# Pair 1's top rows turned by a DMA transpose instead of by the matmul engine, in a Macaron block on one core

## The chip, the cores and the metric
The kernel runs on one core of a Trainium2 chip. Its time is the device time of one launch in microseconds (us). Of the kernel before, three runs gave 824.76, 825.32 and 825.58 us; the median is 825.32.

## What is computed
x has 2 x 1024 rows of 512 numbers. Two feed-forward steps stand around one attention step, each behind a layernorm:

```python
x = x + 0.5 * ffn(layernorm(x))
x = x + attn(layernorm(x))            # one head of 128, softmax over 1024 keys
x = x + 0.5 * ffn(layernorm(x))
# ffn: (silu(x @ Wg) * (x @ Wu)) @ Wd
# Wg, Wu: 512 x 1376, Wd: 1376 x 512, 4-bit weights with group scales and zeros
```

## The kernel before, in words
The 2048 rows are taken 512 at a time (an "x tile" t, four slices r of 128 rows). Two x tiles make a pair: tiles 0 and 1 are pair 0, tiles 2 and 3 pair 1. The first feed-forward step is pairs 0 and 1, then come the attention tiles 4 to 7, and the second feed-forward step is pairs 2 and 3 (tiles 8 to 11). Every fp32 product is made of three passes over a high and a low part (`passes`, `PASSES`), so each operand of the matmul engine is first split: ScalarE copies the high part, VectorE or GpSimd subtracts it and writes the low part.

Pair 0 is computed plainly. Its second half (`plain_bottom`) takes the 11 blocks i of 128 hidden columns: a gate product, an up product, then silu on ScalarE and the product `h` on VectorE. Beside it runs another job, the making of the weight sums for the later pairs: for each of the 11 weight blocks j (`T_ORDER`: the last block first), SyncE fetches the unpacked weights into `full` (`load_full(j)`, L664), VectorE and GpSimd make `t13` and `t24` (`first_blocks(j)`, `second_blocks(j)`), these are split, and SyncE stores them (`save_t(j)`, L671). VectorE makes `first_blocks(10)`, the last, after the last `h` and ahead of the low part of hidden block 2 of the down product (`plain_lo(1, 2)`). Every engine works its instructions off in the order in which they are written, SyncE's DMA queue too.

The rest of pair 0 is `bottom(0)`, the down product: 11 blocks of 12 matmuls. Between them stand two groups of transposes for pair 1 (`turn_pair(1, 0)` after block 4 and `turn_pair(1, 1)` after block 7). Pairs 1 to 3 use a scheme of seven products on sums of quarter blocks: A11 and A12 are the two column halves of the top x tile (t = 2 for pair 1), A21 and A22 those of the bottom tile (t = 3); each quarter block has two halves kt. For each kt ScalarE splits off the high parts (`tiles_hi`), VectorE makes the sums S1 to S4 and low parts (`x_sum`, `x_lo`, `sum_lo`), GpSimd the low parts of S1 and S2. Then VectorE adds pair 0's residual (`residual(0, 1)`, four instructions on `xres`, L2027), and pair 1 begins: `product_1`, `product_6`, `product_2`, and `product_7`, which waits for VectorE's `middle`, the first sum `u2` of pair 1.

A second way to turn x is in the kernel already, for tiles 4, 5, 10 and 11 (`PLANED`): the normalised rows are copied as two planes of 16-bit halves (`to_planes`, GpSimd), the planes are stored to DRAM (`store_planes`, L633), and one DMA transpose per tile brings them back turned into `xn` (`turn_planes`, L638).

Of the kernel before, what the change touches and what calls it, by code (L numbers as in the profile page):

```python
# [11 lines left out]
U16 = mybir.dt.uint16  # L12
# [4 lines left out]
P = 128  # L17
TOKENS, HID, INTER = 2048, 512, 1376
PACK, BITS, GROUP = 8, 4, 128
ROWS = 512  # L20
RT = ROWS // P
# [22 lines left out]
A21 = 7  # L44
# [1 line left out]
PAIRS = 4  # L46


PLANED = (4, 5, 10, 11)

UNITS = 3 * NT
QSLOTS = 6
# [7 lines left out]


TURN_HALVES = tuple((what, kt) for what in (A21, A22, A11, A12) for kt in range(2))
TURN_TILES = tuple((what, kt) for kt in range(2) for what in (A21, A11, A22, A12))
SPLIT_HALVES = tuple((what, kt) for what in (A22, A11, A12) for kt in range(2))
SPLIT_TILES = tuple((what, kt) for kt in range(2) for what in (A11, A22, A12))
SUM_HALVES = tuple((what, kt) for what in (S1, S3, S2, S4) for kt in range(2))
# [11 lines left out]
def macaron(nc, x, w_qkv, b_qkv, w_o, b_o, packed, scales, zeros, g_idx, ident, shifts, groups, out):  # L78
    ctx = ExitStack()
    with ctx:  # L80
# [5 lines left out]
        def place(name, shape, dtype, offset=None):  # L86

            t = nc.alloc_sbuf_tensor_at(name, shape, dtype, offset=at[0] if offset is None else offset)
            if offset is None:
                at[0] += -(-size_of(shape, dtype) // 32) * 32  # L90
            return t
# [82 lines left out]
        wi = place("wi", [P, HID], BF16, t24_at)  # L174


        planes_first = [place(f"planes_first{n}", [P, 2, HID], U16, at_) for n, at_ in enumerate((t13_at, t24_at))]


# [115 lines left out]
        def sem(name):  # L295
            return ctx.enter_context(nc.semaphore(name))
# [26 lines left out]

        s_silu, s_rhi, s_whi, s_th13, s_th24, s_p1, s_g1, s_g2, s_hhi, s_x21, s_xhi, s_shi = (
            sem(n) for n in ("s_silu", "s_rhi", "s_whi", "s_th13", "s_th24", "s_p1", "s_g1", "s_g2", "s_hhi", "s_x21", "s_xhi", "s_shi"))
        s_ahi, s_qhi, s_qkvhi, s_exp, s_phi, s_ohi, s_out, s_planes = (
            sem(n) for n in ("s_ahi", "s_qhi", "s_qkvhi", "s_exp", "s_phi", "s_ohi", "s_out", "s_planes"))

        s_unp, s_int, s_wf, s_tab, s_oh, s_h, s_rlo, s_t13, s_tlo13 = (
            sem(n) for n in ("s_unp", "s_int", "s_wf", "s_tab", "s_oh", "s_h", "s_rlo", "s_t13", "s_tlo13"))  # L330
# [17 lines left out]
        def plane_rows(t, r):  # L348

            if r == 0:  # L350
                return planes_first[t % 2][:, :, :]
            return xn[:, t % 2, r - 1, :].bitcast(U16).rearrange("p (h c) -> p h c", h=2)

        def planes_made(t, r):
            return RT * PLANED.index(t) + r + 1

        def rows_loaded(t):
            return d_row[t % 2], 16 * ((t + 1) // 2)

        def planes_stored(t):  # L360
            return d_planes[t % 2], 16 * RT * (PLANED.index(t) // 2 + 1)

        def planes_turned(t):
            return d_xT[t % 2], 16 * (PLANED.index(t) // 2 + 1)

        def turned_rows(t, k):

            return xn[:, t % 2, k, :]
# [7 lines left out]

        ROWS_TURNED = 6 * KT

        def turned(q, what, kt):
            return 8 + TURN_TILES.index((what, kt)) + 1 if q == 1 else ROWS_TURNED + TURN_HALVES.index((what, kt)) + 1
# [5 lines left out]

            return 2 * (q - 1) + kt + 1 + (2 if what == A11 else 0)

        def block_rows(what):

            return 10 + (what in (A21, A22))

        def turned_block(what, kt):
            return turned_rows(block_rows(what), kt + (2 if what in (A12, A22) else 0))

        def heads_split(a, j):

# [209 lines left out]
        def _(sp):  # L609
# [3 lines left out]
            def load_residual(k, dram, first, slots=range(RT)):  # L613
                for r in slots:

                    if k:
                        sp.wait_ge(d_st[r], 16 * k)
                    sp.dma_start(xres[:, r, :], dram[first + r * P:first + (r + 1) * P, :]).then_inc(d_res[r], 16)
# [10 lines left out]

            def store_planes(t):  # L630
                for r in range(RT):
                    sp.wait_ge(s_planes, planes_made(t, r))
                    sp.dma_start(planes[t][r * P:(r + 1) * P, :, :], plane_rows(t, r)).then_inc(d_planes[t % 2], 16)  # L633

            def turn_planes(t):
# [106 lines left out]
            load_full(2)  # L742
            save_t(0)
            store_rows(0, stream, 0)
            load_residual(1, x, ROWS)
            for j in range(1, NT):
                if j + 2 < NT:
                    load_full(j + 2)
                save_t(j)

            sp.wait_ge(s_up, 2 * NT)
            for i in (NT - 4, NT - 3, NT - 2, NT - 1):
# [15 lines left out]
            for n in range(NT - 2):  # L768
                if n == 0:

                    sp.wait_ge(s_turn, turned(1, A12, 1))
                    stored(0)
                    load_rows(4, stream, 0)
                    stored(1)
                    load_rows(5, stream, ROWS)
                load_block(n + 2)
                if n in (6, 8):
                    store_planes(4 if n == 6 else 5)
                if n == 7:
                    turn_planes(4)  # L780
# [81 lines left out]
        def _(pe):  # L862
# [261 lines left out]
                        turn_pair(1, 1)  # L1124

            def turn_pair(q, kt):
                pe.wait_ge(s_ln[2], RT)
                pe.wait_ge(s_ln[3], RT)
                if kt:
                    pe.wait_ge(s_x21, copied(q, 0))  # L1130
                turn_block(q, A21, kt)
                if kt:
                    pe.wait_ge(s_xlo, split(q, A11, 0))
                turn_block(q, A11, kt)
                if kt:
                    pe.wait_ge(s_xlo, split(q, A22, 0))
                turn_block(q, A22, kt)
                if kt:
                    pe.wait_ge(s_xlo, split(q, A12, 0))
                turn_block(q, A12, kt)  # L1140

            pe.wait_ge(d_small, 32)
            keep_warm(3)
# [223 lines left out]
        def _(act):  # L1367
# [7 lines left out]
                                   scale=rstd[:, t % 2, r:r + 1]).then_inc(s_ln[t], 1)  # L1375


            def rows_hi(t):
                for k in range(KT):
                    act.wait_ge(s_turn, KT * t + k + 1)  # L1380
                    bank = TURN_BANK[k] if t else 4 + k
                    copy((xT0, xT1)[t][:, 0, k, :], ps[:, bank, :]).then_inc(s_rhi, 1)
# [49 lines left out]
            def plain_bottom():  # L1432
                for i in range(NT):
                    w = width(i)
                    if i == NT - 1:

                        act.wait_ge(s_up, 2 * NT)
                    act.wait_ge(s_gate, NT + i + 1)
                    if i == NT - 4:

                        act.wait_ge(d_kept[NT - 1], ALL_KEPT)
                    act.activation(hidden(i)[0:w, :], ps[0:w, plain_bank(1, i, 0), :], ACT.Silu).then_inc(s_silu, 1)
                    if i == NT - 1:

                        act.wait_ge(s_t13, NT - 1)
                        act.wait_ge(s_t24, 2 * (NT - 1))
                        plain_hi(1, 1)

                    if i:
                        t_blocks_hi(i - 1)  # L1450
                    if i in (5, 6, 8, 9):
                        ln_apply(2 if i < 7 else 3, (0, 1) if i in (5, 8) else (2, 3))
                    if i == 3:
                        plain_hi(1, 0)
                plain_hi(1, 2)
                t_blocks_hi(NT - 1)
# [7 lines left out]
                copy(blk_f[:, S2, 1, kt, :], ps[:, turn_at(2, A11, kt), :]).then_inc(s_x21, 1)  # L1464

            def x_hi(q, what, kt):
                if q == 3:
                    act.wait_ge(*planes_turned(block_rows(what)))
                    src = turned_block(what, kt)
                else:  # L1470
                    act.wait_ge(s_turn, turned(q, what, kt))
                    src = ps[:, turn_at(q, what, kt), :]
                copy(blk[:, what, 0, kt, :], src).then_inc(s_xhi, 1)
# [98 lines left out]
            def t_hi(a, kts):  # L1572

                for k in kts:
                    if a < 2:
                        act.wait_ge(*planes_turned(4 + a))
                        src = turned_rows(4 + a, k)
                    else:
                        act.wait_ge(s_turn, 16 + KT * (a - 2) + k + 1)
                        src = ps[:, TURN_BANK[k], :]  # L1580
                    copy(x_turned(a)[:, 0, k, :], src).then_inc(s_ahi, 1)

# [190 lines left out]
        def _(dve):  # L1773
# [39 lines left out]
            def x_sum(q, what, kt):  # L1813
                def turned_tile(which):

                    if q == 3:
                        dve.wait_ge(*planes_turned(block_rows(which)))
                        return turned_block(which, kt)
                    dve.wait_ge(s_xhi, split(q, which, kt))
                    return ps[:, turn_at(q, which, kt), :]  # L1820

# [25 lines left out]
            def x_lo(q, what, kt):  # L1847
                dve.wait_ge(s_xhi, split(q, what, kt))
                if q == 2 and what == A11:

                    dve.wait_ge(s_x21, copied(2, kt, A11))
                src = turned_block(what, kt) if q == 3 else ps[:, turn_at(q, what, kt), :]
                minus(blk[:, what, 1, kt, :], src, f32(blk[:, what, 0, kt, :])).then_inc(s_xlo, 1)

            def sum_lo(q, what, kt):
# [432 lines left out]
        def _(pool):  # L2288
# [15 lines left out]
            def to_planes(t, tiles=range(RT)):  # L2304

                for r in tiles:
                    if r == 0:

                        if t >= 6:
                            pool.wait_ge(*planes_stored(PLANED[PLANED.index(t) - 2]))  # L2310
                    else:

                        pool.wait_ge(s_planes, planes_made(t, r - 1))
                    pool.wait_ge(s_ln[t], r + 1)
                    pool.tensor_copy(plane_rows(t, r), xn[:, t % 2, r, :].bitcast(U16).rearrange("p (c h) -> p h c", h=2)).then_inc(s_planes, 1)

            def w_lo(u):
                pool.wait_ge(s_whi, u + 1)
# [157 lines left out]
```

## Time and profile before
| what | value |
|---|---|
| median of three runs | 825.32 us |
| the profiled execution | 824.82 us |
| its span, first to last instruction | 822.9 us |
| PE (matmul) busy | 809.3 us, 98% |
| DVE (VectorE) busy | 494.3 us, 60% |
| ACT (ScalarE) busy | 272.5 us, 33% |
| POOL (GpSimd) busy | 271.8 us, 33% |
| granted clock of PE | full in all 40 slices |

PE is the matmul engine, PEld its weight loads, SPq the DMA queue of SyncE. In a list of events a row gives start and duration in us, the engine, the line, the operation with what it writes and reads, how many are merged, and in brackets how long the engine was idle before and what ended the wait. The span is 1.9 us shorter than the execution's own time.

### The profile page before, as it was taken

What the parts mean: (1) busy time and instruction counts of PE and PEld (TensorE: products, weight loads), DVE (VectorE), ACT (ScalarE), POOL (GpSimd) and SP (SyncE); (2) the same over time, 40 slices, a digit from 0 to 9 for tenths busy, and PEclk for the clock granted to TensorE, in tenths of its full rate; (3) what the DMA queues carried; (4) which work ended last, traced back from release to release, by engine and by line L of the source; (5) the groups of instructions that cost most, each with busy time, mean ns of one, the idle gap of its engine ahead of it and who ended that gap; (6) DMA issues with size and microseconds to landing.
All of it is one profiled execution on the core that took longest, in us unless ns stands there. A gap on an engine that the chain in (4) does not pass through costs nothing. (4 is left out here: it accounts for less than half of the span.)

```text
span 822.9 us, 10477 instructions
## 1 busy us (share of the span) xinstructions
PE 809.3 (98%) x3868; PEld 665.1 (81%) x3868; DVE 494.3 (60%) x809; ACT 272.5 (33%) x469; POOL 271.8 (33%) x219
## 2 busy tenths in 40 slices
PE   5999999999999999999999999999999999999998
PEld 4877778878888888788898888888878788888786
DVE  7889945756654543557766896546347743443452
ACT  3433433555211211343656872121123321211221
POOL 6646614651115363203064371064431110110100
PEclk9999999999999999999999999999999999999999
DMA  6899958965754467344053159644767164444131
GB/s 168 261 342 288 325 188 278 348 261 231 266 188 160 135 205 201 102 153 154 1 176 131 40 179 356 232 145 159 233 188 225 52 213 159 133 168 133 29 104 52
DMA packets 92221, 151.43 MB, mean 184 GB/s; under 512 B 42860, under 2 KB 53796, under 8 KB 87178
## 3 DMA queue, kind: packets, MB, share of 16 engines
q1 hardware_dynamic: 85492, 139.36, 50.8%
q10 hardware_dynamic: 5814, 7.17, 2.5%
q0 software_dynamic: 864, 4.23, 2.0%
q8 instruction: 31, 0.51, 0.3%
q14 instruction: 20, 0.16, 0.1%
HBM read 104.30 MB, written 42.17 MB: 178 GB/s over the span
## 5 line engine op out<-in xcount | busy, mean ns | idle before, releaser
L868 PE MATMUL ps<-blk,ring 128*128 128x512 f32 (+1 forms) x1386 | 320.8, 389 | 0.0
L868 PEld LDWEIGHTS ps<-blk,ring 128*128 128x128 f32 (+1 forms) x1386 | 256.7, 185 | 57.9 <-POOL blk L2290 0.3
L875 PE MATMUL ps<-wd,hT 128*128 128x512 f32 (+1 forms) x1056 | 250.8, 391 | 0.4 <-DVE hT L1775 0.3
L875 PEld LDWEIGHTS ps<-wd,hT 128*128 128x128 f32 (+1 forms) x1056 | 197.3, 188 | 43.1 <-DVE hT L1775 0.8
L2355 POOL TENSOR_TENSOR h<-h,u 128x512 f32<-128x512 f32 (+1 forms) x33 | 42.7, 1294 | 300.1 <-ACT h L1505 300.1
L875 PE MATMUL ps<-xT,wp 128*128 128x512 f32 x480 | 114.3, 394 | 0.1
L875 PEld LDWEIGHTS ps<-xT,wp 128*128 128x128 f32 x480 | 91.0, 190 | 20.0 <-issue 0.7
L1778 DVE TENSOR_TENSOR u<-ps,p1s 128x512 f32<-128x512 f32 (+1 forms) x66 | 45.3, 687 | 95.7 <-PE ps L868 95.7
L1505 ACT ACTIVATE h<-h 128x512 f32<-128x512 f32 (+1 forms) x33 | 20.9, 632 | 176.9 <-DVE h L1778 176.9
L1778 DVE TENSOR_TENSOR h<-ps,p1s 128x512 f32<-128x512 f32 (+1 forms) x33 | 22.8, 690 | 63.9 <-PE ps L868 63.9
L1778 DVE TENSOR_TENSOR u<-ps,u 128x512 f32<-128x512 f32 (+1 forms) x66 | 45.6, 691 | 24.6 <-PE ps L868 23.5
L1775 DVE TENSOR_TENSOR hT<-h,hT 128x512 fp32r<-128x512 f32 (+1 forms) x44 | 31.5, 727 | 24.2 <-ACT hT L1369 24.1
L1500 ACT ACTIVATE g<-ps 128x512 f32<-128x512 f32 (+1 forms) x33 | 19.7, 598 | 75.0 <-PE ps L868 75.0
L1369 ACT ACTIVATE hT<-u 128x512 fp32r<-128x512 f32 (+1 forms) x33 | 20.9, 632 | 64.5 <-DVE u L2002 64.5
L2002 DVE TENSOR_TENSOR u<-u,g 128x512 f32<-128x512 f32 (+1 forms) x33 | 39.9, 1208 | 1.1
L1369 ACT ACTIVATE hT<-h 128x512 fp32r<-128x512 f32 (+1 forms) x44 | 27.0, 628 | 38.0 <-PE ps L875 37.9
L2301 POOL TENSOR_SCALAR xn<-xn,mv,rstd 128x512 f32<-128x512 f32 x18 | 38.3, 2136 | 0.5
L2295 POOL TENSOR_TENSOR rstd<-rstd,mhalf 128x4 f32<-128x4 f32 (+1 forms) x13 | 15.1, 1158 | 67.7 <-DVE rstd L1797 67.7
L1775 DVE TENSOR_TENSOR hT<-u,hT 128x512 fp32r<-128x512 f32 (+1 forms) x33 | 23.0, 698 | 23.0 <-ACT hT L1369 23.0
L2027 DVE SCALAR_TENSOR_TENSOR xres<-ps,xres 128x512 f32<-128x512 f32 x32 | 21.6, 689 | 24.8 <-PE ps L875 17.4
L2290 POOL TENSOR_TENSOR blk<-blk_f,blk 128x512 fp32r<-128x512 f32 x12 | 18.1, 1516 | 38.9 <-ACT blk L1369 33.6
L1786 DVE BATCH_NORM_STATS2 stats<-xn 128x6 f32<-128x512 f32 x48 | 30.0, 678 | 0.0
(142 smaller groups left out, 897.5 us busy)
## 6 DMA issues: line engine op xcount, KB each, us to landing
ring<-wsaved SPq DMA_DIRECT2D x29, 1024.0 KB, 5.2
ring<-wsaved SPq DMA_DIRECT2D x33, 768.0 KB, 4.6
wsaved<-wp SPq DMA_DIRECT2D x10, 1024.0 KB, 4.9
stream<-xres SPq DMA_DIRECT2D x32, 256.0 KB, 2.3
xn<-stream SPq DMA_DIRECT2D x8, 1024.0 KB, 6.8
xres<-stream SPq DMA_DIRECT2D x32, 256.0 KB, 3.2
wfull<-wf ACTq DMA_DIRECT2D x20, 256.0 KB, 5.6
wsaved<-wp SPq DMA_DIRECT2D x10, 512.0 KB, 5.1
```

Source lines behind the costliest of these rows:

```text
L868: mm = pe.matmul(ps[0:w, bank, :], ring[:, slot, which, a, kt, 0:w], blk[:, which, b, kt, :], start=not onto and kt == 0 and n == 0, stop= ...
L875: mm = pe.matmul(bank_ap, lhs(a), rhs(b), start=first and n == 0, stop=last and n == 2)
L1369: return act.activation(dst, src, ACT.Copy)
L1500: act.activation(g1[0:w, n % 2, :], ps[0:w, product_bank(n // NT + 1, 0), :], ACT.Silu).then_inc(s_g1, 1)
L1505: act.activation(hidden(i)[0:width(i), :], hidden(i)[0:width(i), :], ACT.Silu).then_inc(s_g2, 1)
L1775: return dve.tensor_tensor(out=dst, in0=a, in1=b, op=ALU.subtract)
L1778: return dve.tensor_tensor(out=dst, in0=a, in1=b, op=ALU.add)
L1786: dve.bn_stats(stats[:, t % 2, r, :], x_rows(t)[:, r, :]).then_inc(s_bn, 1)
L2002: dve.tensor_tensor(out=u2[0:w, n % 2, :], in0=u2[0:w, n % 2, :], in1=g1[0:w, n % 2, :], op=ALU.mult)\
L2027: dve.scalar_tensor_tensor(out=xres[:, r, :], in0=ps[:, down_bank(q, half, r), :], scalar=0.5, in1=xres[:, r, :], op0=ALU.mult, op1=ALU.ad ...
L2301: pool.tensor_scalar(x_rows(t)[:, r, :], x_rows(t)[:, r, :], mv[:, t % 2, r, 0:1], rstd[:, t % 2, r:r + 1], ALU.subtract, ALU.mult).then_i ...
L2355: pool.tensor_tensor(out=hidden(i)[0:w, :], in0=hidden(i)[0:w, :], in1=u3[0:w, n % 2, :], op=ALU.mult).then_inc(s_h2, 1)
```

## The change
x tile 2 (A11 and A12 of pair 1) is added to `PLANED`. Its planes are made by ScalarE in `plain_bottom` at i = 5 and 6, behind the layernorm of the same slices; the plane of slice 0 lies in the place of `xres`. SyncE stores them after `save_t(6)`, and turns them after `save_t(7)`. The four loads of the residual rows of pair 0's second half, which stood behind `store_rows(0)`, stand behind that transpose. `turn_pair` turns A21 and A22 alone; ScalarE and VectorE read A11 and A12 from `xn` in SBUF, where they read PSUM before. The plane counters become one per parity of t.

```diff
-PLANED = (4, 5, 10, 11)
+PLANED = (2, 4, 5, 10, 11)
-TURN_TILES = tuple((what, kt) for kt in range(2) for what in (A21, A11, A22, A12))
+TURN_TILES = tuple((what, kt) for kt in range(2) for what in (A21, A22))
+        planes_early = place("planes_early", [P, 2, HID], U16, xres_at)
+        def by_dma(q, what):
+            return q == 3 or q == 1 and what in (A11, A12)
@@ SyncE, pair 0's second half
             store_rows(0, stream, 0)
-            load_residual(1, x, ROWS)
             for j in range(1, NT):
                 if j + 2 < NT:
                     load_full(j + 2)
                 save_t(j)
+                if j == 6:
+                    store_planes(2)
+                if j == 7:
+                    turn_planes(2)
+                    load_residual(1, x, ROWS)
...
                 if n == 0:
-                    sp.wait_ge(s_turn, turned(1, A12, 1))
+                    sp.wait_ge(s_xlo, split(1, A12, 1))
                     stored(0)
@@ matmul engine
             def turn_pair(q, kt):
-                pe.wait_ge(s_ln[2], RT)
                 pe.wait_ge(s_ln[3], RT)
                 if kt:
                     pe.wait_ge(s_x21, copied(q, 0))
                 turn_block(q, A21, kt)
                 if kt:
-                    pe.wait_ge(s_xlo, split(q, A11, 0))
-                turn_block(q, A11, kt)
-                if kt:
                     pe.wait_ge(s_xlo, split(q, A22, 0))
                 turn_block(q, A22, kt)
-                if kt:
-                    pe.wait_ge(s_xlo, split(q, A12, 0))
-                turn_block(q, A12, kt)
@@ ScalarE
+            def to_planes(t, tiles):
+                for r in tiles:
+                    if r == 0:
+                        act.wait_ge(d_st[0], 16)
+                    else:
+                        act.wait_ge(*planes_made(t, r - 1))
+                    act.wait_ge(s_ln[t], r + 1)
+                    copy(plane_rows(t, r), xn[:, t % 2, r, :].bitcast(U16).rearrange("p (c h) -> p h c", h=2)).then_inc(s_planes[t % 2], 1)
...
                     if i in (5, 6, 8, 9):
                         ln_apply(2 if i < 7 else 3, (0, 1) if i in (5, 8) else (2, 3))
+                    if i in (5, 6):
+                        to_planes(2, (0, 1) if i == 5 else (2, 3))
...
             def x_hi(q, what, kt):
-                if q == 3:
-                    act.wait_ge(*planes_turned(block_rows(what)))
-                    src = turned_block(what, kt)
+                if by_dma(q, what):
+                    act.wait_ge(*planes_turned(block_rows(q, what)))
+                    src = turned_block(q, what, kt)
@@ VectorE, x_lo (x_sum alike)
-                src = turned_block(what, kt) if q == 3 else ps[:, turn_at(q, what, kt), :]
+                src = turned_block(q, what, kt) if by_dma(q, what) else ps[:, turn_at(q, what, kt), :]
```

SyncE's queue in pair 0's second half, before, from `load_full(9)` on (`full<-wfull` is a `load_full`, `wsaved<-wp` a `save_t`, `ring<-wsaved` pair 1's first weights):

```order
L664 DMA full<-wfull 128x1024
L671 DMA wsaved<-wp 128x2048
L664 DMA full<-wfull 128x1024
L671 DMA wsaved<-wp 128x2048 x3
L690 DMA ring<-wsaved 128x2048
```

The same place after, from `load_full(8)` on (`xres<-` are the residual loads):

```order
L672 DMA full<-wfull 128x1024
L679 DMA wsaved<-wp 128x2048
L641 DMA planes<-planes_early 128x1024
L641 DMA planes<-xn 128x1024 x3
L672 DMA full<-wfull 128x1024
L679 DMA wsaved<-wp 128x2048
L646 DMA_TRANSPOSE xn<-planes 128x4x1024
L626 DMA xres<-in_L_attn_x 128x512 x4
L672 DMA full<-wfull 128x1024
L679 DMA wsaved<-wp 128x2048 x3
```

Four plane stores, a transpose and four residual loads now stand between `load_full(8)` and `load_full(10)`, the last one.

VectorE in the second group (kt = 1) of pair 1's blocks, before (`blk_f<-...` are the sums, `blk<-...` the low parts):

```order
L1778 TENSOR_TENSOR blk_f<-ps,blk_f 128x512
L1775 TENSOR_TENSOR blk_f<-ps,blk_f 128x512
L1775 TENSOR_TENSOR blk_f<-blk_f,ps 128x512
L1775 TENSOR_TENSOR hT<-h_52,hT 96x512
L1775 TENSOR_TENSOR blk<-ps,blk 128x512 x2
L1775 TENSOR_TENSOR blk_f<-ps,blk_f 128x512
L1775 TENSOR_TENSOR blk<-ps,blk 128x512
L1775 TENSOR_TENSOR blk<-blk_f,blk 128x512 x2
L2027 SCALAR_TENSOR_TENSOR xres<-ps,xres 128x512 x4
```

The same place after:

```order
L1797 TENSOR_TENSOR blk_f<-ps,blk_f 128x512
L1794 TENSOR_TENSOR blk_f<-xn,blk_f 128x512
L1794 TENSOR_TENSOR blk_f<-blk_f,xn 128x512
L1794 TENSOR_TENSOR hT<-h_52,hT 96x512
L1794 TENSOR_TENSOR blk<-xn,blk 128x512
L1794 TENSOR_TENSOR blk<-ps,blk 128x512
L1794 TENSOR_TENSOR blk_f<-xn,blk_f 128x512
L1794 TENSOR_TENSOR blk<-xn,blk 128x512
L1794 TENSOR_TENSOR blk<-blk_f,blk 128x512 x2
L2046 SCALAR_TENSOR_TENSOR xres<-ps,xres 128x512 x4
```

The order of the work is the same; five operands come from `xn` in SBUF in place of `ps` in PSUM.

## Rows read from the trace of the kernel before

**Rows 1.** The page: span, and busy time of the matmul engine.
```profile
span 822.9 us, 10477 instructions
PE 809.3 (98%) x3868; PEld 665.1 (81%) x3868; DVE 494.3 (60%) x809; ACT 272.5 (33%) x469; POOL 271.8 (33%) x219
```

**Rows 2.** Timeline of PE, 186 to 216 us: start, duration, what.
```profile
190.33 1.91 PE L886 MATMUL ps<-idt,xn 128*128 128x128 f32 x16
191.99 8.43 PE L875 MATMUL ps<-wd,hT 128*128 128x512 f32 x36
200.26 1.91 PE L886 MATMUL ps<-idt,xn 128*128 128x128 f32 x16
...
210.24 6.08 PE L868 MATMUL ps<-blk,ring 128*128 128x512 f32 x26
```

**Rows 3.** Timeline of SyncE's DMA queue, 100 to 220 us.
```profile
134.98 2.33 SPq L618 DMA_DIRECT2D xres<-in_L_attn_x  x4
...
164.07 0.32 SPq L671 DMA_DIRECT2D wsaved<-wp  x1
165.70 0.32 SPq L664 DMA_DIRECT2D full<-wfull  x1
...
170.27 0.32 SPq L664 DMA_DIRECT2D full<-wfull  x1
```

**Rows 4.** The same queue, at the transposes of tiles 4 and 5.
```profile
294.26 1.90 SPq L633 DMA_DIRECT2D planes<-xn  x3
...
306.03 5.92 SPq L638 DMA_TRANSPOSE xn<-planes  x1
...
326.41 4.13 SPq L638 DMA_TRANSPOSE xn<-planes  x1
```

**Rows 5.** All four DMA transposes, from issue to landing.
```profile
DMA to landing us min/median/max: 6.2/7.9/8.0
```

**Rows 6.** DMA issues: count, size, median us to landing; whole span.
```profile
full<-wfull SPq DMA_DIRECT2D x10, 512.0 KB, 4.6
...
planes<-xn SPq DMA_DIRECT2D x12, 256.0 KB, 5.7
```

**Rows 7.** The same of 134 to 146 us alone.
```profile
full<-wfull SPq DMA_DIRECT2D x2, 512.0 KB, 7.8
```

**Rows 8.** Busy time by stretch, granted clock, DMA share, GB/s.
```profile
155.00:160.00 5.00, 5.00 (x24) 4.14 (x23) 3.96 (x11) 3.23 (x6) 4.18 (x5) 1.00 0.89 318
```

**Rows 9.** ScalarE, exponentials of attention: count, busy, mean ns of one.
```profile
L1631 ACT ACTIVATE pr<-ps,nmx 128x1024 f32<-128x1024 f32 x16 | 17.8, 1113 | 7.1 <-DVE nmx L2130 6.7
```

**Rows 10.** Timeline of DVE, 165 to 270 us (the first: 143 to 146).
```profile
144.03 0.69 DVE L1775 TENSOR_TENSOR t<-full 128x512 f32<-128x512 f32 x1 [4.44 <-DMA full<-wfull]
...
179.18 1.62 DVE L1775 TENSOR_TENSOR t<-full 128x512 f32<-128x512 f32 x1
180.71 0.68 DVE L1775 TENSOR_TENSOR hT<-h,hT 128x512 fp32r<-128x512 f32 x1
...
202.57 0.69 DVE L1778 TENSOR_TENSOR blk_f<-ps,blk_f 128x512 f32<-128x512 f32 x1 [1.65 <-ACT blk L1369]
...
205.10 1.28 DVE L1775 TENSOR_TENSOR blk<-ps,blk 128x512 fp32r<-128x512 f32 x2
...
209.82 2.47 DVE L2027 SCALAR_TENSOR_TENSOR xres<-ps,xres 128x512 f32<-128x512 f32 x4
213.25 0.69 DVE L1778 TENSOR_TENSOR u<-ps,p1s 128x512 f32<-128x512 f32 x1 [0.97 <-PE ps L868]
```

**Rows 11.** Timeline of POOL, 165 to 300 us: the first low part of kt = 1.
```profile
204.73 1.62 POOL L2290 TENSOR_TENSOR blk<-blk_f,blk 128x512 fp32r<-128x512 f32 x1 [6.16 <-ACT blk L1369]
```

**Rows 12.** Timeline of DVE at pair 3's blocks, all from `xn`, 622 to 662 us.
```profile
631.17 0.68 DVE L1778 TENSOR_TENSOR blk_f<-xn 128x512 f32<-128x512 f32 x1
...
633.76 2.38 DVE L1775 TENSOR_TENSOR blk<-xn,blk 128x512 fp32r<-128x512 f32 x2
...
640.78 0.68 DVE L1778 TENSOR_TENSOR blk_f<-xn 128x512 f32<-128x512 f32 x1
```

More of the change, by code:

```diff
@@ L325, in macaron @@
             sem(n) for n in ("s_silu", "s_rhi", "s_whi", "s_th13", "s_th24", "s_p1", "s_g1", "s_g2", "s_hhi", "s_x21", "s_xhi", "s_shi"))
-        s_ahi, s_qhi, s_qkvhi, s_exp, s_phi, s_ohi, s_out, s_planes = (
-            sem(n) for n in ("s_ahi", "s_qhi", "s_qkvhi", "s_exp", "s_phi", "s_ohi", "s_out", "s_planes"))
+        s_ahi, s_qhi, s_qkvhi, s_exp, s_phi, s_ohi, s_out = (
+            sem(n) for n in ("s_ahi", "s_qhi", "s_qkvhi", "s_exp", "s_phi", "s_ohi", "s_out"))
+        s_planes = [sem(f"s_planes{n}") for n in range(2)]
         s_unp, s_int, s_wf, s_tab, s_oh, s_h, s_rlo, s_t13, s_tlo13 = (
@@ L350, in plane_rows, with of_parity @@
             if r == 0:
-                return planes_first[t % 2][:, :, :]
+                return (planes_early if t == 2 else planes_first[t % 2])[:, :, :]
             return xn[:, t % 2, r - 1, :].bitcast(U16).rearrange("p (h c) -> p h c", h=2)
+        def of_parity(t):
+            return [u for u in PLANED if u % 2 == t % 2].index(t)
         def planes_made(t, r):
-            return RT * PLANED.index(t) + r + 1
+            return s_planes[t % 2], RT * of_parity(t) + r + 1
         def rows_loaded(t):
@@ L360, in planes_stored @@
         def planes_stored(t):
-            return d_planes[t % 2], 16 * RT * (PLANED.index(t) // 2 + 1)
+            return d_planes[t % 2], 16 * RT * (of_parity(t) + 1)
         def planes_turned(t):
-            return d_xT[t % 2], 16 * (PLANED.index(t) // 2 + 1)
+            return d_xT[t % 2], 16 * (of_parity(t) + 1)
         def turned_rows(t, k):
@@ L375, in hidden @@
             return h2_back[:, NT - 1 - i, :]
-        ROWS_TURNED = 6 * KT
+        ROWS_TURNED = 5 * KT
         def turned(q, what, kt):
@@ L389, in copied, with block_rows, turned_block @@
             return 2 * (q - 1) + kt + 1 + (2 if what == A11 else 0)
[L391 to L396, printed above, removed]
+        def by_dma(q, what):
+            return q == 3 or q == 1 and what in (A11, A12)
+        def block_rows(q, what):
+            return {1: 2, 3: 10}[q] + (what in (A21, A22))
+        def turned_block(q, what, kt):
+            return turned_rows(block_rows(q, what), kt + (2 if what in (A12, A22) else 0))
         def heads_split(a, j):
@@ L631, in store_planes @@
                 for r in range(RT):
-                    sp.wait_ge(s_planes, planes_made(t, r))
+                    sp.wait_ge(*planes_made(t, r))
                     sp.dma_start(planes[t][r * P:(r + 1) * P, :, :], plane_rows(t, r)).then_inc(d_planes[t % 2], 16)
@@ L1578, in t_hi @@
                     else:
-                        act.wait_ge(s_turn, 16 + KT * (a - 2) + k + 1)
+                        act.wait_ge(s_turn, 12 + KT * (a - 2) + k + 1)
                         src = ps[:, TURN_BANK[k], :]
@@ L1814, in turned_tile @@
                 def turned_tile(which):
-                    if q == 3:
-                        dve.wait_ge(*planes_turned(block_rows(which)))
-                        return turned_block(which, kt)
+                    if by_dma(q, which):
+                        dve.wait_ge(*planes_turned(block_rows(q, which)))
+                        return turned_block(q, which, kt)
                     dve.wait_ge(s_xhi, split(q, which, kt))
@@ L2309, in to_planes @@
                         if t >= 6:
-                            pool.wait_ge(*planes_stored(PLANED[PLANED.index(t) - 2]))
+                            pool.wait_ge(*planes_stored(t - 6))
                     else:
-                        pool.wait_ge(s_planes, planes_made(t, r - 1))
+                        pool.wait_ge(*planes_made(t, r - 1))
                     pool.wait_ge(s_ln[t], r + 1)
-                    pool.tensor_copy(plane_rows(t, r), xn[:, t % 2, r, :].bitcast(U16).rearrange("p (c h) -> p h c", h=2)).then_inc(s_planes, 1)
+                    pool.tensor_copy(plane_rows(t, r), xn[:, t % 2, r, :].bitcast(U16).rearrange("p (c h) -> p h c", h=2)).then_inc(s_planes[t % 2], 1)
             def w_lo(u):
```

## The prediction, made before the changed kernel ran
> **What bounds the kernel now.** I read the page first: the matmul engine is busy 98% of the span [rows 1], and its clock was granted in full [rows 8]. So what is taken from this engine's stream counts in full, and what makes it wait does too; work elsewhere counts only where it ends last. The timeline of that engine comes next: at 190.33 and at 200.26 us stand the two groups of 16 transposes that the change halves, with 36 matmuls of the down product behind each, and the first product of pair 1 starts at 210.24 [rows 2]. The reader is to see that nothing idles between these rows. The timelines of SyncE's queue and of VectorE show what must be ready by then [rows 3, 4, 10].
>
> **What is removed: 16 of 32 transposes.** The next matmul starts 191.99 - 190.33 = 1.66 us after 16 transposes began, 0.104 us each [rows 2]. Sixteen go, eight per group, as no other has to be added on this engine: 16 x 0.104 = 1.66 us. This is the whole of what the change can give here, 0.2% of the time. The waits that guarded their PSUM banks go too, but the engine did not idle there.
>
> **ScalarE: four copies of 1024 numbers.** The trace has no such copy on this engine. The nearest row is the exponential of 128x1024 at 1113 ns [rows 9]; I take 1.1 us each, 4.5 us in all, 2.2 us in block 5 and 2.2 in block 6. ScalarE was busy 3.23 of 5 us at 155 to 160 us [rows 8], which holds its two layernorm slices, so a block of 5.4 us nearly fills. The matmul engine asks for the `h` of two blocks ago, so a slip of up to 5 us costs it nothing; cost 0, with the planes made near 158 us. Were the copies at twice the length, they would still be ready near 162 us, about when SyncE comes to them.
>
> **The residual loads, moved.** Before, VectorE idled 4.44 us until 144.03 for weights [rows 10] that were fetched behind the residual's four loads, issued over 2.33 us from 134.98 [rows 3]. With those gone the weight sums of blocks 3 to 6 come sooner. It is no gain on the matmul engine, but `save_t(6)`, issued at 164.07 before [rows 3], should be issued at about 161.6. I keep 164.1 as the late end.
>
> **SyncE's queue: the last weight fetch comes late.** `load_full(10)` was issued at 170.27 [rows 3]. Now it stands behind four plane stores, the transpose's wait for their landing, the transpose, and four residual loads. Step by step: `save_t(6)` at 161.6; the plane stores take some 1.9 us [rows 4], the last issued by 163.5; landing 5.7 us [rows 6], 169.2; the transpose holds the queue 5.92 us with other traffic, 4.13 with little [rows 4], and this stretch is busy at a DMA share of 0.89 [rows 8], so 175.1; the residual 2.33 [rows 3], so `load_full(10)` is issued at 177.5. It lands 4.6 us later at the median [rows 6], 7.8 in the crowded stretch from 134 us [rows 7]. A full megabyte of residual and the end of the transpose stand right ahead: 1.5 MB at 318 GB/s [rows 8] are 4.9 us, and I take 5.7, so it lands at 183.2.
>
> When is it needed? VectorE took it up at 179.18 and was ready for the low part of hidden block 2 at 180.71 [rows 10]; it works in order. That block's matmuls, the last 36 before 190.33 at 0.23 us each, begin at 182.1 [rows 2]. An uncontended `t` and the low part take 0.61 + 0.68 = 1.3 us, so a landing up to 180.8 costs nothing, and each microsecond behind that is one of the matmul engine. At 183.2: 2.4 us lost. The bounds: issue with the short transpose, and landing in 4.6, gives 161.6 + 1.9 + 5.7 + 4.13 + 2.33 + 4.6 = 180.3, cost 0; the late `save_t(6)`, 5.92 and 7.8 give 164.1 + 1.9 + 5.7 + 5.92 + 2.33 + 7.8 = 187.8, cost 7.0. Behind that one the same block's other steps (two low parts on VectorE, `t24` on GpSimd) have more room than they need, and the stores `save_t(8)` to `save_t(10)`, also later, are wanted by pair 1's first weights only, 15 us on.
>
> In the trace a DMA transpose lands 6.2 to 8.0 us after its issue [rows 5]. The Trainium skill (DMA: Bandwidth & Descriptors, Latency and other measured facts) gives a transpose with strided rows 261 GB/s effective, which for 1 MB is an estimate of 4.0 us. By that the queue would be free some 2 us sooner and the loss nearer 0.5 us; no row here is as short.
>
> **VectorE: operands from SBUF.** A collision is bought here. In pair 3, where all blocks come from `xn`, the pair of low parts takes 2.38 us from 633.76 [rows 12]; in pair 1, from PSUM, it takes 1.28 from 205.10, though GpSimd works from 204.73 to 206.35 [rows 10, 11]. So 1.1 us is added per group kt. The Trainium skill (SBUF — State Buffer, Who interferes with whom) says that a `tensor_tensor` with both inputs in SBUF and a GpSimd instruction that reads SBUF block each other for the whole instruction; the two rows agree.
>
> Where does that end? Before, between the first sum of kt = 1 (202.57) and the end of the residual (209.82 + 2.47 = 212.29) VectorE worked 9.72 us on end, and then idled 0.97 us for the matmuls of `product_6` [rows 10]. After, the two groups' starts lie 0.83 us closer (8 transposes less): 9.93 - 0.83 = 9.10 us [rows 2], but a group with the collision keeps VectorE for 640.78 - 631.17 = 9.61 us [rows 12]. Counted from the start of the second group's transposes, its first sum stood at 2.31 us; it would stand at about 2.9. Then 9.72 + 1.1, and the first sum of pair 1, 0.69: `u2` is there at 14.45. `product_7` could start three products (18 matmuls, 4.1 us) behind the first one, and that one starts at 210.24 - 200.26 - 0.83 = 9.15: 13.25 [rows 2]. The matmul engine waits 1.2 us. Bounds: 0, if GpSimd and VectorE miss each other, and 2.3, if the residual's end is hit a second time by 1.1 us. I take 1.2.
>
> **Sum.** -1.66 + 2.4 + 1.2 = +1.9 us on the profiled execution's 824.82, which is 826.8; that execution lay 0.5 us under the median of the three runs, so against 825.32 I forecast 827.3 us.
>
> **The rivals.**
> (a) The fetch is in time, and only the collision stays: -1.66 + 1.2 = -0.5, 824.9 us, on the not-slower side. With the collision at 1.2 us the sign turns at a landing of 181.3. For it speaks the lower bound of 180.3 just under the 180.8 needed; against it every median in the chain.
> (b) Neither wait appears: -1.66, 823.7 us. For it: before, the matmul engine waited almost nowhere, and VectorE had 1.65 and 0.97 us idle around these places. Against it: pair 3's rows show the collision with the same order of work.
> (c) The fetch is very late, because the transpose shares the DMA engines with the stores of megabytes: landing at 186 or later, +5.2 and more, with 1.2 and -1.66 that is +4.7, 830 us and above. For it speaks the 7.8 us landing in the crowded stretch [rows 7]; against it that ScalarE and VectorE should be ahead of before by then.
> (d) The fetch is late but the collision is missed: -1.66 + 2.4, 826.1 us.
>
> **Chances.** The forecast, both waits at about these sizes, 0.50; (a) 0.17; (b) 0.10; (c) 0.13; (d) 0.10. What a measurement here can tell from no change is 0.2%, 1.65 us. Faster than 823.7 is only half of (b) and some of (a)'s lower edge: 0.10. The slow side, above 827.0, has (c) and two thirds of the forecast's case: 0.47. The rest, 0.43, is no change that can be told. My range is 824.2 to 830.2 us; the forecast's own case is 825.8 to 829.2.
>
> **What would show it.** In the profile after: PE has two groups of 8 transposes, 0.83 us each; the row of `t<-full` for the last block starts at 183 rather than 179 with "<-DMA full", and the matmuls of `hT` wait on DVE `hT` for 2 to 3 us right behind; the queue shows the last `full<-wfull` at 177 to 178; DVE's pair of low parts takes 2.4 us in both groups, and PE waits near its 19th to 24th matmul of pair 1 for DVE `u`. I am wrong on the first wait if that fetch is issued before 175 us, on the second if `u` starts less than 0.3 us behind the end of `product_6`, and altogether if PE waits nowhere between 176 and 215 us.

## The result and the profile after

| | median, us | runs | ratio to before, 95% interval |
|---|---|---|---|
| before, same chip | 825.24 | 5 | |
| after | 830.38 | 5 | 1.0068 [1.0053, 1.0082] |

The change makes the kernel 5.1 us slower, 0.6 to 0.7%. My forecast was 827.3, with 830.2 as the upper edge: the direction was right, the size was not. The profiled execution took 830.38 us, its span is 5.6 us longer than before. The page of after, against [rows 1]:

```profile
span 828.5 us, 10458 instructions
PE 810.4 (98%) x3852; PEld 664.2 (80%) x3852; DVE 495.1 (60%) x809; ACT 276.3 (33%) x473; POOL 271.6 (33%) x219
```

Sixteen matmul instructions fewer (3852 for 3868), and yet the engine is busy a microsecond longer. Waits of PE after (us in total, times, longest), those that before did not have at this size:

```profile
PE ps L887 <- DVE hT L1794: 3.3, 3, 2.8
...
PE ps L880 <- DVE u L1797: 0.7, 1, 0.7
PE ps L880 <- POOL blk L2309: 0.5, 1, 0.5
```

Timeline of PE after, from the down product of pair 0 on; it answers to [rows 2]:

```profile
176.75 6.03 PE L887 MATMUL ps<-wd,hT 128*128 128x512 f32 x24
185.52 9.79 PE L887 MATMUL ps<-wd,hT 128*128 128x512 f32 x36 [2.75 <-DVE hT L1794]
195.15 1.03 PE L898 MATMUL ps<-idt,xn 128*128 128x128 f32 x8
195.94 8.43 PE L887 MATMUL ps<-wd,hT 128*128 128x512 f32 x36
204.20 1.04 PE L898 MATMUL ps<-idt,xn 128*128 128x128 f32 x8
205.46 8.48 PE L887 MATMUL ps<-wd,hT 128*128 128x512 f32 x36 [0.22 <-DVE hT L1794]
213.78 4.27 PE L880 MATMUL ps<-blk,ring 128*128 128x512 f32 x18
218.70 12.53 PE L880 MATMUL ps<-blk,ring 128*128 128x512 f32 x54 [0.65 <-DVE u L1797]
```

The groups of transposes are 8 each and take 0.79 us instead of 1.66. In front of them stands a wait of 2.75 us; behind it, 36 matmuls take 195.15 - 185.52 = 9.63 us, where they take 8.26 to 8.32 in the two other places of this trace, and 8.27 before. The granted clock tells why (stretch, PE busy, granted clock, DMA share, GB/s):

```profile
183.00:184.00 1.00, 0.00 (x0) 1.00 1.06 446
185.00:186.00 1.00, 0.48 (x1) 0.50 1.00 418
187.00:188.00 1.00, 1.00 (x4) 0.50 0.41 172
188.00:189.00 1.00, 1.00 (x5) 0.80 0.10 41
```

0.50 is 1.2 GHz, the lower of the engine's two levels: it stood idle from 182.8 us, and when it went on at 185.52 it ran some 3 us at the lower level. SyncE's queue, against [rows 3]:

```profile
161.82 0.32 SPq L679 DMA_DIRECT2D wsaved<-wp  x1
...
162.67 3.34 SPq L641 DMA_DIRECT2D planes<-xn  x3
166.18 0.53 SPq L672 DMA_DIRECT2D full<-wfull  x1
167.26 0.33 SPq L679 DMA_DIRECT2D wsaved<-wp  x1
168.69 6.48 SPq L646 DMA_TRANSPOSE xn<-planes  x1
175.22 2.70 SPq L626 DMA_DIRECT2D xres<-in_L_attn_x  x4
178.08 0.33 SPq L672 DMA_DIRECT2D full<-wfull  x1
```

`load_full(10)`, the last row, is issued 7.8 us later than before. VectorE waits for it, and then meets the collision; against [rows 10]:

```profile
184.17 0.69 DVE L1794 TENSOR_TENSOR t<-full 128x512 f32<-128x512 f32 x1 [4.64 <-DMA full<-wfull]
184.78 0.69 DVE L1794 TENSOR_TENSOR hT<-h,hT 128x512 fp32r<-128x512 f32 x1
...
209.66 1.79 DVE L1794 TENSOR_TENSOR blk<-xn,blk 128x512 fp32r<-128x512 f32 x1
...
215.48 2.47 DVE L2046 SCALAR_TENSOR_TENSOR xres<-ps,xres 128x512 f32<-128x512 f32 x4
217.88 0.67 DVE L1797 TENSOR_TENSOR u<-ps,p1s 128x512 f32<-128x512 f32 x1
```

The row at 184.78 is what the matmul engine waited for. The low part at 209.66 takes 1.79 us, where 0.68 is the rule, and the residual and `u` come right behind it with no idle time: VectorE is the bound there. ScalarE's copies, the part that I cost at nothing:

```profile
150.87 1.04 ACT L1374 ACTIVATE planes_early<-xn 128x1024 uint16<-128x1024 uint16 x1
...
155.94 2.13 ACT L1374 ACTIVATE xn<-xn 128x1024 uint16<-128x1024 uint16 x2
```

They are done at 158.1 us, SyncE comes for them at 162.2, and no engine waits.

### The profile page after: what moved, and what is told of

It is laid out like the page before. It is cut to its first block and busy times, and to the rows that moved or that the text cites. A ratio compares the mean times of both kernels' runs of the same rounds, so it can differ in the third digit from the quotient of the medians.

```text
span 828.5 us, 10458 instructions
## 1 busy us (share of the span) xinstructions
PE 810.4 (98%) x3852; PEld 664.2 (80%) x3852; DVE 495.1 (60%) x809; ACT 276.3 (33%) x473; POOL 271.6 (33%) x219
## 5 line engine op out<-in xcount | busy, mean ns | idle before, releaser
L2309 POOL TENSOR_TENSOR wp<-wf,wp 128x512 fp32r<-128x512 f32 x20 | 26.6, 1331 | 11.7 <-ACT wp L1374 11.4
```

The source lines that it names most:

```text
L2309: return pool.tensor_tensor(out=dst, in0=a, in1=b, op=ALU.subtract)
```

## The experiments

The theory after reading the trace of after, "Q": the last weight fetch, late in SyncE's queue, costs 3.0 us, the lower clock behind this wait 1.3, and VectorE's collision 1.3; the transposes give back 1.7. Its rivals: the added traffic rather than the order ("T"), and the SBUF operands as the main loss ("C").

### e1: the transpose behind the last fetch
```diff
-                if j == 7:
+                if j == 8:
                     turn_planes(2)
                     load_residual(1, x, ROWS)
```


> The changed kernel with the transpose of tile 2 and the four residual loads one step later in SyncE's queue: behind load_full(10) and save_t(8), where they stood behind save_t(7). Theory Q (the queue): the changed kernel loses its time because load_full(10), issued at 178.1 us, lands at 184.2 where 180.8 would have done; the matmul engine then starts hidden block 2 about 3.0 us late, and runs the first 3 us after that wait at half the granted clock, 1.3 us more. With the fetch issued near 170 us both go: no wait of DVE t<-full, no matmul wait on DVE hT in front of the third block, granted clock 1.0 throughout, and a time 4.4 us under the changed kernel's, 826.0 us (825.3 to 826.8). Rival T (traffic): it is the additional 4 MB and the transpose themselves that crowd the DMA engines between 160 and 185 us, wherever they stand; then load_full(10) still lands behind 181 us, and the time stays above 828.5. Rival C: the operands from SBUF carry most of the loss; then the time stays above 828.5 as well, but with VectorE never waiting for DMA.

Measured: 825.72 us against 825.43 of before in the same job, ratio 0.9997 [0.9988, 1.0006]. SyncE's queue, then the timelines of PE and of DVE in the trace of e1:

```profile
170.38 0.32 SPq L672 DMA_DIRECT2D full<-wfull  x1
173.30 0.32 SPq L679 DMA_DIRECT2D wsaved<-wp  x1
173.67 7.91 SPq L646 DMA_TRANSPOSE xn<-planes  x1
```
```profile
177.35 14.17 PE L887 MATMUL ps<-wd,hT 128*128 128x512 f32 x60
```
```profile
180.22 1.62 DVE L1794 TENSOR_TENSOR t<-full 128x512 f32<-128x512 f32 x1
```

All 60 matmuls in one row without a wait, `t<-full` without one too, and the clock at 1.0 from 183 to 191 us. One `if` moved by one step takes 4.7 us away (826.0 us was expected). The bytes are the same, so T falls; C falls as the main cause, since the operands are the same.

### e2: three of the four residual loads back in their old place
```diff
             store_rows(0, stream, 0)
+            load_residual(1, x, ROWS, (1, 2, 3))
...
                     turn_planes(2)
-                    load_residual(1, x, ROWS)
+                    load_residual(1, x, ROWS, (0,))
```


> The changed kernel with three of the four residual loads (slices 1 to 3) back behind store_rows(0); only slice 0, whose place the planes use, stays behind the transpose. Theory Q: each microsecond by which load_full(10) lands sooner is one of the matmul engine, and the 2.7 us that four loads hold the queue shrink to 0.7, with 0.75 MB less in front of the fetch. If the chain in front (save_t(6) at 161.8) keeps its time, the fetch lands near 181.5 and the wait shrinks from 3.0 to about 0.7 us, without the half clock: 830.4 - 2.3 - 1.3 = 826.8 us. If the residual in front of load_full(3) delays the chain as in the kernel before (save_t(6) at 164.1), 2 us of this are given back: about 828.5. Rival T: no change within 0.8 us, since the same bytes move.

Measured: 831.84 us, ratio 1.0068 [1.0054, 1.0082]: 3.3 us or more above both cases of Q. The ratio is that of after, so the times do not tell e2 from after, and what e2 shows is read from its trace. SyncE's queue in the trace of e2, then its PE:

```profile
164.75 0.32 SPq L679 DMA_DIRECT2D wsaved<-wp  x1
...
171.59 8.20 SPq L646 DMA_TRANSPOSE xn<-planes  x1
...
180.59 0.32 SPq L672 DMA_DIRECT2D full<-wfull  x1
```
```profile
186.43 11.01 PE L888 MATMUL ps<-wd,hT 128*128 128x512 f32 x36 [3.92 <-DVE hT L1795]
```

With the residual ahead of `load_full(3)`, `save_t(6)` is 2.9 us later (164.75 for 161.82), as I had reckoned for the late case. What I had not: the transpose now holds the queue 8.20 us instead of 6.48. The fetch is issued 2.5 us later than in after, and the wait is 3.92 us instead of 2.75. It agrees with Q (a later fetch, a longer wait). T's "no change within 0.8 us" is missed by the medians (1.5 us) and not by the ratios, so e2 decides nothing against T; e1 does. It also shows that with the residual away from its old place the chain in front runs earlier.

### e3: the wait filled with idle matmuls
```diff
                 down(q, 1, 1)
+                if q == 0:
+                    pe.wait_ge(s_sum, RT)
+                    for _ in range(12):
+                        pe.matmul(ps[:, 7, :], wd[:, 0, 0, 0:P], wd[:, 0, 0, :], start=True, stop=True)
```


> The changed kernel with 12 additional matmuls of 128x512 on the matmul engine (into an unused PSUM bank, nobody reads them) between the down product's second and third block, where it waits. 12 x 0.23 us = 2.7 us of work in a wait of 3.0 us. Theory G (the granted clock fell because the engine stood idle): the wait for the low part of hidden block 2 stays, but nearly empty; the granted clock stays 1.0 behind it, and the 1.3 us of the half clock come back: 829.1 us. Rival: the fall has another cause (the program's place, the DMA load), then the clock is 0.5 behind the wait all the same, and the time is that of the changed kernel or longer, 830.4 to 830.7.

Measured: 828.62 us, ratio 1.0039 [1.0025, 1.0052]: 1.8 us less than after, with 12 more matmuls (829.1 was expected). PE's timeline in e3, then its clock in the stretch:

```profile
182.34 2.88 PE L1130 MATMUL ps<-wd 128*128 128x512 f32 x12
185.14 8.51 PE L887 MATMUL ps<-wd,hT 128*128 128x512 f32 x36
```
```profile
184.00:186.00 2.00, 2.00 (x10) 1.00 0.97 406
```

The fetch is as late as in after, the 36 matmuls behind take 193.48 - 185.14 = 8.34 us, and the clock stays at 1.00 with the DMA engines as busy. So it was the engine's own idle time ahead of the fall, and not the traffic, that cost the 1.3 us. Between the traces of after and e3 the gain is 2.4 us at the start of pair 2's down product: 1.3 from the clock, 0.4 because block 2 starts earlier, 0.7 in the attention part (below).

### e4: transposes left out, nothing else
This is the kernel before, with 12 of its 32 transposes left out, and so a part of the computation.

```diff
-                turn_tile(turn_at(q, what, kt), t, kt + (2 if what in (A12, A22) else 0))
+                turn_tile(turn_at(q, what, kt), t, kt + (2 if what in (A12, A22) else 0),
+                          (RT - 1,) if q == 1 and what in (A11, A12) else range(RT))
```


> The kernel before, with 12 of pair 1's 32 transposes left out and nothing else changed (of A11 and A12 only the last slice of each tile is turned; the rest of these blocks is stale data, so this leaves out part of the computation). It measures the first term by itself. By the rows of before, 12 x 0.104 = 1.25 us; VectorE, with its operands in PSUM as before, has 0.97 us to spare at product_7, which two groups 0.62 us closer use up, but do not exceed by more than 0.3 us. Expected: 1.0 to 1.25 us under the kernel before, 824.1 us. Rival: VectorE's chain from the first group on is already as long as the matmul engine's, and the transposes removed only turn into a wait on DVE u: no gain, 825.2.

Measured: 824.71 us against 825.43, ratio 0.9993 [0.9984, 1.0002]: 0.7 us less, with an interval that just includes no change. I had expected 1.0 to 1.25 us. In the trace the matmul engine does not wait on `u` (VectorE still idles 0.29 us ahead of it, 0.97 before), and pair 1's down product starts here:

```profile
341.08 32.89 PE L875 MATMUL ps<-wd,hT 128*128 128x512 f32 x144
```

Before it was 342.37, so the 12 transposes are worth 1.29 us at that point, 0.107 each. From the first transpose to `product_1` it is 208.94 - 190.34 = 18.60 us instead of 19.91. The median keeps only part of it, because the attention part of e4 is longer (below).

### e6: only the residual loads behind the last fetch
```diff
                 if j == 7:
                     turn_planes(2)
+                if j == 8:
                     load_residual(1, x, ROWS)
```


> The changed kernel with only the four residual loads moved behind load_full(10) and save_t(8); the transpose stays ahead of that fetch. It divides the late fetch between the two. Theory: in the changed kernel the transpose holds the queue for 6.5 us and the residual for 2.9. Without the residual in front, load_full(10) is issued at 175.2 instead of 178.1 us and has 1 MB less ahead of it, so it lands about 2.9 us sooner, at 181.3 in the changed kernel's trace, where the matmul engine needs it at 181.2: the wait shrinks from 2.75 us to under 0.5, too short for the clock to fall, and 2.7 + 1.3 us come back: 826.4 us, 0.7 above e1's 825.7 at most. Rival: the fetch lands when the transpose's transfers are done, whatever stands between; these end 8 us after its issue, at 176.7, and the fetch still needs 5 to 6 us from its own issue: the same 181. A landing at 183 or later, and 829 us or more, would say that the bytes of the stores and the transpose, and not the order, set it.

Measured: 825.88 us against 825.71, ratio 1.0001 [0.9992, 1.0010]. SyncE's queue in the trace of e6, then its DVE:

```profile
175.68 0.44 SPq L672 DMA_DIRECT2D full<-wfull  x1
```
```profile
180.39 0.86 DVE L1795 TENSOR_TENSOR t<-full 128x512 f32<-128x512 f32 x1 [0.84 <-DMA full<-wfull]
```

The fetch lands 4.7 us after its issue, and VectorE waits 0.84 us that it had to spare; the matmul engine does not wait there. To take the four loads away from in front of the fetch is enough: the transpose ahead of it, 6.7 us of the queue, just fits. (I had expected a landing at 181.3 and 826.4 us; the rival expected 181 as well, so this run does not part the two. The transpose alone moved, with the loads left in front, was not tried.) Past the spare time a delay costs at once: 2.4 us earlier at the issue and 3.8 at the landing turn a loss of 4.4 into none.

### e5 and e7: the collision
e5 is e1 with `middle(0)` (the sum `u`) between the second and the third residual instruction; e7 is e5 with block A22 taken before A11.

```diff
+                if q == 0:
+                    residual(q, 1, (0, 1))
+                    middle(0)
+                    residual(q, 1, (2, 3))
@@ e7, VectorE (ScalarE's tiles_hi and SPLIT_TILES alike)
-                            x_lo(q + 1, A11, kt)
                             x_lo(q + 1, A22, kt)
+                            x_lo(q + 1, A11, kt)
```


> The kernel with the transpose behind load_full(10) (e1), and on VectorE the first sum of pair 1, u2, put between the second and third instruction of pair 0's residual instead of behind the fourth. Theory Q with the collision as its second part: in e1 the matmul engine waits 0.63 us in the trace for this sum (product_7 starts 0.84 us late), because VectorE's chain of blocks from SBUF is longer than the matmuls. With the sum ahead of two residual instructions (1.2 us) this wait goes: no wait on DVE u, and 0.8 us less: 824.9 us, against e1's 825.7. Rival: the residual's last two instructions are waited for in turn (the store of xres, the DMA that fetches the next residual), or the sum itself waits for product_6 and holds up VectorE; then no gain, 825.7.

> e5, and in the groups of pair 1 (and pair 3) ScalarE and VectorE take block A22 before A11, so that the VectorE instruction which meets GpSimd's first low part has an operand in PSUM (pair 1) and runs beside it; A11 from SBUF comes when GpSimd is nearly done. Theory: the collision costs VectorE 1.1 us per group in e1 (1.78 instead of 0.68); with the order turned it costs about 0.5. Then the wait of 0.21 us for hT behind the second group of transposes (block 8 starts 0.43 us late) goes too, and the time is 0.4 to 0.5 us under e5: 824.5 us. Rival: GpSimd, which reads SBUF, is pushed back instead, and the second low part or the wait for hT stays: no difference from e5.

Measured: e5 824.59 us, ratio 0.9993 [0.9984, 1.0001]; e7 824.36 us, ratio 0.9989 [0.9981, 0.9998], with 825.39 for before in that job. The low part of A11 at kt = 1, and pair 1's first matmuls, in e5:

```profile
204.46 1.79 DVE L1794 TENSOR_TENSOR blk<-xn,blk 128x512 fp32r<-128x512 f32 x1
```
```profile
208.59 13.79 PE L880 MATMUL ps<-blk,ring 128*128 128x512 f32 x60
```

DVE's timeline at the same place in e7:
```profile
204.60 0.68 DVE L1794 TENSOR_TENSOR blk<-ps,blk 128x512 fp32r<-128x512 f32 x1
205.20 1.19 DVE L1794 TENSOR_TENSOR blk<-xn,blk 128x512 fp32r<-128x512 f32 x1
```

In e5 the wait on `u` is gone (one row of 60 matmuls), and in e7 the one on `hT` too. From the first group of transposes to `product_1` e1 took 210.00 - 191.36 = 18.64 us, e7 209.34 - 191.18 = 18.16, before 19.91. The block with a PSUM operand runs beside GpSimd's low part (204.23 to 205.85 us) at its own 0.68 us, and only the SBUF one is held, to 1.19 us. That agrees with the Trainium skill (SBUF — State Buffer, Who interferes with whom), which names two SBUF inputs as the condition. Not all of e7's gain is the collision: with A22 first the first group's first sum starts 1.9 us behind its first transpose, and 2.4 us in e1. Each of the two steps is smaller than what the medians can tell apart (824.59 and 824.36). That e7 is under before at all, by some 1.0 us, is told by an interval that only just excludes 1; its edit also turns the order in pair 3, and no run parts the two places.

### c1 and c2: before and after once more


> The kernel before once more, for its attention part. From the start of pair 1's down product to that of pair 2's the matmul engine took 278.6 us in the trace of before, but 279.7 us in those of the changed kernel, of e1, e2 and e4, where a wait for GpSimd's blk and one for VectorE's xn stand. Theory P (phase): nothing in the change causes this 1.1 us; the waits come from residual loads that land a little later or earlier against GpSimd's work, and a second trace of before can show 279.7 as well. Theory R: the change causes it (its timeline is shifted against the DMA queue); then before shows 278.6 again.

> The changed kernel once more. Theory P: its attention part takes 278.6 or 279.7 us, as it falls. Theory R: 279.7 again. In both the wait for the last fetch is 2.5 to 3.5 us and is followed by 2.5 to 5 us at half the granted clock.

Measured, one run each: 825.84 and 831.19 us. The wait for the last fetch in c2 is shorter than I expected (2.18 us, expected 2.5 to 3.5), and the clock falls all the same; it reads 0.78 from 186 to 187 us and 0.50 for the two behind:

```profile
185.72 10.09 PE L887 MATMUL ps<-wd,hT 128*128 128x512 f32 x36 [2.18 <-DVE hT L1794]
195.65 1.03 PE L898 MATMUL ps<-idt,xn 128*128 128x128 f32 x8
```

The 36 matmuls take 9.93 us, 1.7 more than 8.27. From the start of pair 1's down product to the start of pair 2's, in the first trace of before and in that of c1:

```profile
342.37 32.89 PE L875 MATMUL ps<-wd,hT 128*128 128x512 f32 x144
...
620.97 27.43 PE L875 MATMUL ps<-wd,hT 128*128 128x512 f32 x120
```
```profile
342.76 32.89 PE L875 MATMUL ps<-wd,hT 128*128 128x512 f32 x144
...
495.12 11.22 PE L868 MATMUL ps<-blk,ring 128*128 128x512 f32 x48 [0.54 <-POOL blk L2290]
...
621.96 27.43 PE L875 MATMUL ps<-wd,hT 128*128 128x512 f32 x120
```

278.60 and 279.20 us: the wait for GpSimd's `blk` comes without any change. The others: after 279.66, c2 279.88, e1 279.83, e2 279.81, e4 279.70, e5 279.84, e6 279.54, e3 278.93, e7 279.12. So 0.6 of the 1.06 us that after loses there can appear without the change. e4 has none of the new transfers and no operand moved to SBUF, and shows the whole 1.1, with the wait for `blk` in it. The new transfers are not needed for it, then. A shifted timeline of the matmul engine (R) is not excluded, as e4's is shifted too, and that residual loads landing against GpSimd's work are the reason (P) is argued, not shown. For the remaining 0.5 two traces of before, at 278.6 and 279.2, do not tell.

## Why the prediction was wrong, point by point

**The transposes, -1.66.** Measured 1.66 - 0.79 = 0.87 us per group, -1.74; right, and e4 shows it by itself (0.107 to 0.109 us each).

**ScalarE, 0.** Right: 1.04 to 1.07 us a copy (forecast 1.1), planes ready at 158.1 (near 158), nobody waits.

**The residual loads moved.** Right: `save_t(6)` at 161.82 (161.6), and e2 shows the other case at 164.75 (164.1).

**The last fetch, +2.4.** The mechanism was right. The chain's times came out within 1.0 us from the transpose on, partly by luck: the plane stores held the queue for 3.8 us instead of 1.9 and landed in 4.1 us at the median instead of 5.7, two misses that nearly cancel. The transpose was issued at 168.7 (169.2) and held the queue 6.48 (5.92), the fetch was issued at 178.1 (177.5), and VectorE took it up at 184.17 (183.2). The matmul engine started block 2 at 185.52. Before, 36 matmuls ahead of 190.33 put that at 182.06, and this run was 0.45 us later already at the down product's start, so 3.0 us were lost instead of 2.4. (The 0.45 stands already at 116 us, ahead of everything that the change moves: the 240 matmuls there start at 116.76, 116.31 before, and 116.72 in c1.)

**The step that failed** is the sentence that each microsecond behind the limit "is one of the matmul engine". I took a wait for its length alone. After 2.75 us of idle time the engine comes back at 1.2 GHz, and the 36 matmuls cost 9.63 - 8.27 = 1.36 us more; with 3.92 us in e2 it is 197.28 - 186.43 - 8.27 = 2.6. e3 shows that the idle time is the cause. The profile of before has no such wait outside the start, so no row of it priced this; the term was missing, and my range had no room for it. A second term that I put at nothing without a reason is the attention part, 1.06 us here; its cause stays open (c1 and e4).

**The collision, +1.2.** Measured: block 8 starts 1.26 us behind the second group's first transpose instead of 0.79 or so, 0.47 us lost at a wait on `hT`, and `product_7` starts 218.70 - 213.78 = 4.92 us behind `product_1` where three products take 4.08: 0.84. Together 1.3. `product_7` starts 218.70 - 204.20 = 14.50 us behind the second group's first transpose, where I had 14.45. I had the whole at `product_7`; a part of it ends at `hT` first: the held low part at 200.12 pushes back a sum, ScalarE waits 2.86 us for it (1.76 before), and its copies of `hT` come behind that. e5 and e7 take both away.

**The rest.** From the first transposes to `product_7` all terms add up: after is 4.38 us late there (218.70 against 210.24 + 4.08), which is 0.45 + 3.0 + 1.36 - 1.74 + 1.3. The attention part adds 1.06 and the rows between 0.1, 5.5 in all at the start of pair 2's down product. The forecast's case counted 1.9 here. Of the 3.6 between (3.1 by the medians), 1.36 are the clock, 1.06 the attention part, 0.6 the longer wait, 0.45 the start (c1 has it without the change), and the last 0.1 to 0.2 the rows between and the collision.

**The rivals.** (a) and (b), no wait for the fetch, are e1 and e5 to e7, not the change. (c), a very late fetch, has the right time with the wrong reason: the fetch landed at 184.2 and not at 186. (d), no collision, is out by the 1.3 us above.

The Trainium skill (DMA: Bandwidth & Descriptors, Latency and other measured facts) would have a transpose of 1 MB done in an estimated 4.0 us. No landing here is as short: the five transposes of after land

```profile
DMA to landing us min/median/max: 6.2/7.9/10.0
```

after their issue, and the one in this crowded stretch is the longest. That is the time from issue to landing and not the transfer alone, so it is the number for a forecast of the wait, and the rate itself is not measured here.

## What to carry to other kernels

Moving work off a saturated engine by way of a queue is worth what the queue's next consumer can wait: look up what stands behind the inserted transfers and when each is needed, and put the insertion behind the last one that has little time to spare (here one `if`, 4.7 us). On an engine that never waits, price a new wait of two to four microseconds at its length and another half to three quarters of it for the clock (three traces here: 1.7 on 2.2, 1.36 on 2.75, 2.6 on 3.92 us). And most of the gain of sixteen transposes (1.7 us) can be eaten by operands that move from PSUM to SBUF (1.3 us), if GpSimd works beside them; take the block that still lies in PSUM at the moment of the collision.

## What the runs showed of the hardware

- After idle waits of 2.2 (c2), 2.75 (after) and 3.92 us (e2) the matmul engine ran at 1.2 GHz for some 3 to 6 us, and the next 36 matmuls cost 1.7, 1.36 and 2.6 us more. With the idle time filled (e3) the clock stayed at 2.4 GHz. Waits of 0.65 us on `u` (after) and of 1.62 us at 50 us (c2) left the granted clock at 1.00.
- A DMA transpose of 1 MB held SyncE's queue for 6.43 to 8.20 us in the eight traces of the changed kernel and its variants (after 6.48, e1 7.91, e2 8.20) where other transfers were in flight, against 4.13 and 5.92 in [rows 4]. Every DMA behind it in the queue is later by that.
- ScalarE copies 128x1024 16-bit numbers, read with a stride of two, in 1.04 us, GpSimd in 1.04 to 1.5.
- VectorE's `blk<-xn,blk`, both inputs in SBUF, took 1.79 us where GpSimd's low part was already running (209.66 against 209.28 us in after), and 0.68 us where it started ahead of GpSimd's (203.01 against 203.24). `blk<-ps,blk` took 0.68 us with GpSimd's already running (e7).
